# A four-layer graph network on one core: order of steps, three smaller steps, and a new setup

## What is computed

```python
# A (layer 0)
e = (x @ a_i)[:, :, None] + (x @ a_j)[:, None, :]
e = (e - mean) * rsqrt(var + 1e-14) * adj + adj      # mean, var of the whole e
alpha = softmax(leaky(e), axis=1); h = sigmoid(alpha @ x)
# B, C (layer 1)
h = x @ Wp + bp; scores = leaky(h @ a_src + (h @ a_dst)^T), no edge -> -max
h_gat = relu(layernorm((softmax(scores) * adj) @ h) * gat_g + gat_b)
h_gin = (1 + eps) * h_gat + adj @ h_gat
z = relu(layernorm(h_gin @ W1 + b1) * mlp_g + mlp_b); relu(z @ W2 + b2 + h_gat)
# D (layer 2)
idx = cumsum(adj > 0) - 1; A = softmax(where(adj > 0, e[idx], NEG), axis=1)
out = (A * I) @ (x @ W[0]) + (A * (1 - I)) @ (x @ W[1]) + bias
# E (layer 3)
h = x @ W; softmax over edges and self loops of leaky(h @ a_src + (h @ a_dst)^T); elu(attn @ h)
```

## Time and profile before

| | |
|---|---|
| median of 3 runs | 1327.42 us (1327.37 to 1328.85) |
| the profiled execution | 1329.5 us |
| its span, first to last instruction | 1327.8 us |
| granted TensorE clock, mean | 0.965 |
| PE, DVE, ACT, POOL busy | 88, 88, 77, 31% of the span |
| instructions | 30557 |
| DMA | 27 GB/s on average |

### The profile page before, as it was taken

One profiled execution on the slowest core, in us unless ns is written; L12 is line 12 of the kernel. 1 busy time (PEld: TensorE's weight loads), 2 busy tenths in 40 slices (PEclk: granted clock), 3 DMA queues, 4 the chain that ended last, 5 costly groups with the idle time before them and its releaser, 6 DMA issues. The chain is left out here.

```text
span 1327.8 us, 30557 instructions
## 1 busy us (share of the span) xinstructions
PE 1167.9 (88%) x8412; PEld 984.1 (74%) x8412; DVE 1163.5 (88%) x4200; ACT 1017.9 (77%) x2548; POOL 408.1 (31%) x831
## 2 busy tenths in 40 slices
PE   4637799999999999999999999999999999999873
PEld 3225578888787788788888777887888787788763
...
GB/s 59 1 27 29 24 25 18 33 32 24 32 32 32 16 24 32 32 32 32 30 25 32 32 32 16 24 32 32 32 32 24 32 32 32 31 11 31 17 9 17
DMA packets 59462, 35.97 MB, mean 27 GB/s; under 512 B 3873, under 2 KB 54817, under 8 KB 59425
## 3 DMA queue, kind: packets, MB, share of 16 engines
...
...
## 5 line engine op out<-in xcount | busy, mean ns | idle before, releaser
L564 POOL TENSOR_TENSOR lnve_Z<-lnmv_Z,consts 128x4 f32<-128x4 f32 x32 | 17.4, 543 | 468.2 <-DVE lnmv_Z L878 468.2
L685 PEld LDWEIGHTS ps<-xsA,pA 128*128 128x128 f32 x1024 | 123.9, 198 | 30.1 <-ACT xsA L1177 28.7
L685 PE MATMUL ps<-xsA,pA 128*128 128x128 f32 x1024 | 131.2, 284 | 10.4 <-ACT xsA L1177 10.4
L750 PE MATMUL ps<-hE,pTE 128*128 128x128 f32 x1024 | 139.5, 280 | 0.6 <-ACT pTE L1269 0.6
L750 PE MATMUL ps<-hB,pTB 128*128 128x128 f32 x1024 | 135.1, 275 | 0.7 <-DVE pTB L921 0.7
L808 PE MATMUL ps<-h1D,att_j 128*128 128x128 f32 x1024 | 135.2, 275 | 0.0
L765 PE MATMUL ps<-gin_j,hgat 128*128 128x512 f32 x256 | 120.6, 615 | 15.9 <-ACT hgat L1240 15.8
L750 PEld LDWEIGHTS ps<-hB,pTB 128*128 128x128 f32 x1024 | 129.3, 192 | 6.9 <-DVE pTB L921 0.9
L750 PEld LDWEIGHTS ps<-hE,pTE 128*128 128x128 f32 x1024 | 125.9, 194 | 3.0 <-issue 0.8
L808 PEld LDWEIGHTS ps<-h1D,att_j 128*128 128x128 f32 x1024 | 127.1, 192 | 1.4
L1167 ACT ACTIVATE pA<-vA,nmA,rirA 128x512 f32<-128x512 f32 x128 | 104.3, 815 | 29.2 <-DVE nmA L985 29.2
...
## 6 DMA issues: line engine op xcount, KB each, us to landing
...
```

The costliest lines, as they stand in the source:

```text
L685: last = mm(at("aggA")[:, i * P:(i + 1) * P], pA[:, j, i * P:(i + 1) * P], xsA[:, j], start=(j == 0), stop=(j == NT - 1))
L750: last = mm(at("agg" + n)[:, i * P:(i + 1) * P], att[n]["pT"][:, i, j], att[n]["h"][:, j, 0:P], start=(j == 0), stop=(j == NT - 1))
```

## The change

The main part:
- All five orders are new, and with them the delays. On DVE the delays were 0 to 5 and are 0 to 4; on PE and ACT they are 1 to 5.
- Steps of DVE that held several dependent instructions are cut into steps of one, so that others can stand between: bn and join (the aggregate), centre_A0 into dots_A0 and dots_A1, centre_A1 into mean_A, centre_A, square_A, variance_A into sumsq_A and variance_A, split_A into shift_A, high_A, rest_A0, middle_A, rest_A1, low_A, max_A and offset_A, gain_B and offset_B, q_C and y_C, y1_E and y_E, zz_B, join_B and stats_B.
- `IN_BANK` is arranged anew for the new orders.
- rows_A makes four transposes instead of eight: the two vectors lie in one 128-wide tile, 32 columns apart, and copy_rowsA takes them out in two copies of 32 partitions. The ones that pair_A needs stand in rowsA for good.
- The t row isn't a product of its own: wx has a second extra column, so h has the value per node, and four transposes of that column, broadcast to 128, make the row. The step then waits for the copies of h.
- D is computed as (A x) W[1] instead of A (x W[1]): `ax_D` takes xD as it is, four products of 512 columns like gin, `copy_axD` replaces copy_hD, `out_D` multiplies by W[1] and adds the diagonal part.

The setup:
- The counts in each row are products on PE, of the transposed mask and an upper triangle, both bf16, instead of scans. The counts are used relative to the row's offset, so that they stay small enough for bf16 (cut at 300), and the offset is a second thin product.
- The row offsets are a product with a 128x128 triangle and sums with ones, on at most four columns each.
- The diagonal is handled only in the four 128x128 blocks on the diagonal: for no3_i, gin_j and the attention. no3_i and gin_j are first copied on ACT.
- adj's transposes need no free bank, each has one. The vectors of weights are two-column products instead of 128-column ones.
- On DVE, the splitting of the biases is interleaved with the softmax of the attention.

```diff
-                for k in range(2 * NT):
-                    last = nc.tensor.transpose(at("rowsA").bitcast(BF16)[:, k * P:(k + 1) * P], sp_tiles[k], identb[:])
+                for k in range(NT):
+                    last = nc.tensor.transpose(at("rowsA").bitcast(BF16)[:, k * P:(k + 1) * P], spA[:, k], identb[:])
...
                 def t_row(g):
-                    pe.wait_ge(s[f"xT{n}_ready"], g.now)
+                    pe.wait_ge(s[f"h012{n}_ready"], g.now)
+                    pe.wait_ge(s[f"h3{n}_ready"], g.now)
                     bank_free(g, "t" + n)
-                    mm(at("t" + n), wt[:], xT[:], start=True, stop=True).then_inc(s[f"t{n}_in_psum"], 1)
+                    for j in range(NT):
+                        last = nc.tensor.transpose(at("t" + n)[:, j * P:(j + 1) * P],
+                                                   att[n]["h"][:, j, P + 1:P + 2].to_broadcast([P, P]), ident[:])
+                    last.then_inc(s[f"t{n}_in_psum"], 1)
...
+                    for j in range(half * NT // 2, (half + 1) * NT // 2):
+                        last = mm(at("axD"), xD[:, j], att2_j[:, j], start=(j == 0), stop=(j == NT - 1))
...
+            def out_D(g):
+                pe.wait_ge(s["axT_ready"], g.now)
+                pe.wait_ge(s["xTdD_ready"], g.now)
+                bank_free(g, "outD")
+                mm(tiles(at("outD")), onesb[:], bias_l2, start=True, stop=False, skip_group_check=True)
+                for i in range(NT):
+                    dst = at("outD")[:, i * P:(i + 1) * P]
+                    mm(dst, axT[:, i * P:(i + 1) * P], l2w1[:], start=False, stop=False, skip_group_check=True)
+                    last = mm(dst, xTdD[:, i * P:(i + 1) * P], l2w0[:], start=False, stop=True, skip_group_check=True)
...
+                rows = at("rowsA").bitcast(BF16)
+                a.copy(rowsA[0:32, 0], rows[0:32, 0:N])
+                a.copy(rowsA[32:64, 1], rows[32:64, 0:N]).then_inc(s["rowsA_ready"], 1)
```

The core of the new setup on PE and DVE:

```diff
+                for i in range(NT):
+                    for t in range(NT):
+                        last = mm(counts[:, i, t * P:], maskT[:, t, i * P:(i + 1) * P], upto[:, t, t * P:],
+                                  start=(t == 0), stop=(t == NT - 1), skip_group_check=True)
+                    last.then_inc(s["counts_in_psum"], 1)
...
+                mm(ps[:, 0, 0:NT], above[:], tot[:], start=True, stop=False, skip_group_check=True)
...
+                        one = sel_i[:, i, c * P:(c + 1) * P]
+                        mm(ps[:, 4 + c], one, cnt[:, i], start=(i == 0), stop=(i == NT - 1))
+                        last = mm(ps[:, 6 + c, 0:1], one, offb[:, i:i + 1], start=(i == 0), stop=(i == NT - 1))
...
+                def softmax_in(i):
+                    dve.wait_ge(s["vals_in_psum"], i + 1)
+                    dve.wait_ge(s["tmp_ready"], NT)
+                    v.tensor_tensor_reduce(out=vals[:, i], in0=ps[:, 4 + i], in1=tmp[:, i], scale=1.0, scalar=3e38,
+                                           op0=ALU.add, op1=ALU.min, accum_out=rowm[:, i:i + 1]).then_inc(s["rowm_ready"], 1)
+
+                def softmax_out(i):
+                    block = vals[:, i, i * P:(i + 1) * P]
+                    dve.wait_ge(s["exp2_ready"], i + 1)
+                    then(v.reciprocal(rowr[:, i:i + 1], rowz[:, i:i + 1]), "rowr_ready")
+                    then(v.tensor_scalar(vals[:, i], vals[:, i], rowr[:, i:i + 1], None, ALU.mult), "scaled")
+                    then(v.tensor_tensor(dia[:, i], block, ident[:], ALU.mult), "dia_ready")
+                    v.tensor_tensor(block, block, dia[:, i], ALU.subtract).then_inc(s["vals_ready"], 1)
```

More of the change, by code:

```diff
@@ L334, in _ @@
+                pool.wait_ge(s["no3_ready"], NT)
                 pool.wait_ge(s["weights_in"], 16 * N_LOADS)
@@ new lines, in _ @@
+                dve.wait_ge(s["tot_ready"], 1)
+                dve.wait_ge(s["off_in_psum"], 1)
+                then(v.tensor_copy(off[:], ps[:, 0, 0:NT]), "off_ready")
+                v.tensor_copy(offb[:], off[:]).then_inc(s["offb_ready"], 1)
+                v.tensor_scalar(thr[:], off[:], -1.0, float(EDGES + 1), ALU.mult, ALU.add).then_inc(s["thr_ready"], 1)
+                then(v.tensor_tensor(nxt[:], off[:], tot[:], ALU.add), "nxt_ready")
+                dve.wait_ge(s["k_ready"], 2)
@@ L427, in _ @@
                 for i in range(NT):
[L428 to L429 removed]
+                    v.tensor_scalar(ge_i[:, i], kf[:], off[:, i:i + 1], None, ALU.is_ge).then_inc(s["ge_ready"], 1)
                 for i in range(NT):
[L431 removed]
@@ L925, in _, with dots_A, step @@
             mult_B0, mult_B1, mult_B2, mult_B3 = (mult_B(i) for i in range(NT))
-            def centre_A0(g):
-                dve.wait_ge(s["xA_in"], 16 * g.now)
-                for c in range(2):
+            def dots_A(c):
+                def step(g):
+                    if c == 0:
+                        dve.wait_ge(s["xA_in"], 16 * g.now)
+                        dve.wait_ge(s["cenA_ready"], g.last)
                     for t in range(NT):
@@ new lines, in turn @@
+                t.run(square_A, 0)
+                t.run(bn_A, 1)
+                t.run(sumsq_A, 0)
+                t.run(variance_A, 0)
+                t.run(gain_B, 2)
+                t.run(join_A, 1)
+                t.run(shift_A, 0)
+                t.run(high_A, 0)
+                t.run(offset_B, 2)
+                t.run(rest_A0, 0)
+                t.run(middle_A, 0)
+                t.run(rest_A1, 0)
+                t.run(L_E0, 4)
+                t.run(low_A, 0)
+                t.run(L_E1, 4)
@@ L1287, in turn @@
             def turn(t):
-                t.run(copy_h3B, 2)
-                t.run(copy_ginT, 3)
+                t.run(y2_E, 5)
+                t.run(relu_B, 3)
+                t.run(copy_axD, 4)
+                t.run(copy_rowsA, 1)
+                t.run(copy_xTD, 4)
+                t.run(norm_A, 2)
+                t.run(exp_E0, 5)
+                t.run(copy_ginT, 3)
+                t.run(copy_xTB, 2)
+                t.run(exp_E1, 5)
+                t.run(copy_pE0, 5)
+                t.run(exp_E2, 5)
```

603 lines of the change are left out of this document (308 added, 295 removed), and 5 rows, old and new, of tables (IN_BANK, READ_BY).

## The result

The change makes the kernel faster: 1248.61 us median (1246.97 to 1253.42) against 1327.39, a ratio of 0.941 (95% interval 0.938 to 0.944). The prediction was 1234, with a range of 1205 to 1278: inside, 14.6 us above the forecast.

The account below looks back on a forecast made before the run. DVE was taken as the bound. Setup 56.6 us, 31 turns of 34.09 less 22 for filling (1034.8) and 143 at the end gave a span of 1234.4, median 1234.0 us; range 1215 to 1255 (0.57), outer 1205 to 1278.

Parts of the forecast that it names:

- PE's forecast: PE's busy time per turn: from 34.5 to 33.4 us at most, leaving 0.7 us of room with DVE still the bound.
- Dependent neighbours: DVE's turn: instructions reading their neighbour's result cost 2.41 us before and 0.70 in the new order, a gain of 1.71.
- The lock over xTdD: DVE instructions held beside POOL's xTdD product: 0.98 us a turn before, 0.78 after, a gain of 0.20.
- Waits: DVE's waits per turn: 1.03 us before, 0.45 after by laying steps end to end; gain 0.58, bounds +1.03 and -1.0.
- called met: DVE's L_E0 would find its input ready: it stands at 6.6 us in the turn, y2_E through at 6.45.
- The rival of waits that return: Turn: waits of 1.0 us as before and two instructions held by xTdD; turn 35.3 us, total 1271; chance 0.19.
- The turn's sum: One turn: 36.58 - 1.71 - 0.58 - 0.20 = 34.09 us.
- a turn without waits and without the lock: Better rival for the turn: xTdD holds nothing and waits vanish; turn 33.2 us, total 1206; chance 0.13.
- Filling: First turns, lighter than later ones: 21, 28, 31 and 33 us, saving 22 us instead of 41.9 before.
- Setup: Before the main part: long steps gone or moved to ACT, first load near 50 us; gain 20 us, bounds 14 and 25.
- The end: Behind the last veA: 159.1 us becomes 143, with B steps closer together and shorter chains for the last graph.
- The slower rival: ACT's queue from norm_B to copy_rowsA: a late norm_B delays v_A0 each turn; at 4 us lost, 1358; chance 0.05.

Follow-up runs that it names:

- Experiment 8: The kernel after, with the t rows of both attentions made by 128x512 f32 products again as before the change: 1248.71 us in one run.
- Experiment 1: The kernel after, with the aggregates of A, Z, C, D and E put back right behind their bn_stats on DVE: 1287.72 us, ratio 0.968.
- experiment 2: The kernel after, with DVE's loop edge moved from in front of stats_B to behind y_E, order of work kept: 1244.3 us, ratio 0.935.
- Experiment 7: The kernel after, with POOL running power_A ahead of rstd_E instead of behind it: 1363.5 us in one run.

## Why the prediction was right, and where it was off

- **What bounds the kernel.** DVE, as read from the earlier trace rows. Experiment 8 gave PE 0.8 us more a turn at no cost. PE's forecast, 33.4 us at most, came out at 32.9.
- **Dependent neighbours, -1.71 us.** Right. Six such places are left as counted, and 0.15 us more is lost behind bn_D, where q_C follows. Experiment 1 shows that putting only the aggregates back costs 1.14 us a turn.
- **The lock over xTdD, -0.20.** Right in kind, mis-sized twice. The loss after was 0.35 and not 0.78, since v_A0 passes and only M_E2 is held: gross gain 0.63. But 0.42 us lay hidden under the lock before, the loop edge, of which 0.31 show after (booked below, with the waits). The prediction took the whole 0.98 as gone and named nothing that would be late next in its place.
- **Waits, -0.58.** The step that failed: 1.42 us and not 0.45. v_A0 was forecast at 0.15 late and is 0.22. shift_A was forecast at 0.1 and is 0.53: the layout put POOL's power at veA with 1.0 us, and left out that rstd_E stands ahead of it in POOL's queue, lengthened there beside DVE's y_A and t1B (lnve_E 0.66 and lnnb_E 0.68 us where others take 0.20). But the queue is the smaller part. In experiment 2 POOL is free, the power starts 0.32 us behind the start of veA and takes 0.99, and shift_A still costs 0.38, 0.15 less. L_E0 was called met, with y2_E through at 6.45, and is 0.36; 0.10 of it is norm_E, which waits for the same rstd_E; the other 0.26 is a gap without a releaser, 0.17 with the loop written out. The third is the loop edge, 0.31, for which the layout had no term. The rival of waits that return, with 1.0 us, was nearer here, and overrated the lock.
- **The turn's sum.** With the sizes measured, 36.58 - 1.71 + 0.15 (behind bn_D) - 0.63 (the lock) + 0.39 (waits, the loop edge among them) makes 34.78, and the turn is 34.49. Laid side by side, DVE's two turns show what the sum leaves out: before, gaps around rzE and mult_B0 of 0.17 together that were never booked and are gone; after, 0.10 in front of prA and 0.03 at meanA. The other 0.25 us of gain lies in many instructions that are 0.01 to 0.03 us shorter in the new order (y_C 0.692 before and 0.660 after, y_E 0.692 and 0.659); why isn't shown.
- **Two rivals in numbers.** With the prediction's own terms, a turn without waits and without the lock is 36.58 - 1.71 - 1.03 - 0.98 = 32.86 and not 33.2. Waits as before and two held instructions at 35.3 has 0.4 more for the lock than before, of which the rows show 0.29 at most (1.27 against 0.98). Neither moves the forecast.
- **Filling, 22 us.** 18.1: the first turns took 21.8, 31.4, 33.4 and 32.6 us, against 21, 28, 31 and 33, which by themselves would have saved 23.4.
- **Setup, -20 us.** -21.5. The first load is issued at 48.5. The forecast of its steps held within a microsecond or so: adj transposes 6.3 to 9.9, counts through at 16.2 (forecast 15.1), selections at 21.9 (21.4), edge products at 26.5 (26.5), vals at 36.6 (36), the last softmax step at 42.7 (43.7). The 16 products of vals took 8.89 us against 8.3 by L371. The counts were priced at 1.2 GHz, 4.3 us, and took 4.45; the granted clock that the profile gives for that stretch is 1.00, so the size came out, and the profile doesn't bear out the reason.

```profile
6.29 3.65 PE L342 MATMUL ps<-ident,adj_i 128*128 128x128 f32 x16 [6.29 <-DMA adj_i<-in_adj_dram]
11.70 4.45 PE L349 MATMUL ps<-vA 128*128 128x512 bf16 x16 [1.76 <-DVE vA L417]
27.74 8.89 PE L390 MATMUL ps<-pTE 128*128 128x512 f32 x16
```

- **The end, 143 us.** 141.9. For graph 31, answering:

```profile
1137.80 0.69 DVE L1062 SCALAR_TENSOR_TENSOR y_A<-thA,xrA 128x512 f32<-128x512 f32 x1 [1.70 <-ACT thA L1274]
1144.39 1.66 ACT L1213 ACTIVATE xB<-y_A,lnnb_A,lnr_A 128x128 f32<-128x128 f32 x4
1151.99 1.41 DVE L928 SCALAR_TENSOR_TENSOR wB<-ps,hB,y2B 128x512 f32<-128x512 f32 x2 [1.77 <-ACT y2B L1290]
1168.77 1.51 ACT L1213 ACTIVATE nB<-ps,lnnb_B,lnr_B 128x128 f32<-128x128 f32 x4
```

From the first wB to nB 16.8 us (forecast 18.4, before 28.6), from y_A to xB 6.6 (7.7, before 13.0), from veA to y_A 31.6 (32.0).

- **The slower rival.** In the kernel after it didn't decide: copy_rowsA starts at 4.79 us, and v_A0 waits 0.14. Experiment 7, which makes norm_E 2.8 us late, doesn't test it either: there copy_rowsA waits for rows_A and not in ACT's queue.
